# Decoder layer on one core: late maximum units of the local steps issued in pairs, value product behind them, query projection behind the value product

## The reference, cut to what matters

```python
def local_attention(x):                 # 16 heads of 8, windows of 64 tokens
    q, k, v = split(layernorm(x) @ w_qkv)
    # a chunk of 64 queries sees its own chunk and the one before it
    scores = qc @ kcat.T / 8 ** 0.5     # causal inside the window
    return softmax(scores) @ vcat @ w_out

def cross_attention(x, ctx):            # 16 heads of 8, all 256 context tokens
    q, k, v = layernorm(x) @ Wq.T + bq, ctx @ Wk.T + bk, ctx @ Wv.T + bv
    return softmax(where(mask, q @ k.T / 8 ** 0.5, -1e8)) @ v @ Wo.T + bo

x = x + local_attention(x)
x = x + cross_attention(x, ctx)
x = x + ffn(x)      # 8-bit and ternary quantised, depthwise convolution, silu
```

## Time and profile before

| what | us |
|---|---|
| median of 3 runs | 323.36 |
| lowest and highest | 322.66, 327.88 |
| the profiled execution's own time | 324.95 |
| its span, first to last instruction | 323.2 |

### The profile page before, as it was taken

One profiled execution on the slowest core, in us unless ns is written; L12 is line 12 of the kernel. 1 busy time (PEld: TensorE's weight loads), 2 busy tenths in 40 slices (PEclk: granted clock), 3 DMA queues, 4 the chain that ended last, 5 costly groups with the idle time before them and its releaser, 6 DMA issues.

```text
span 323.2 us, 8541 instructions
## 1 busy us (share of the span) xinstructions
PE 285.6 (88%) x3298; PEld 183.8 (57%) x3298; DVE 231.3 (72%) x562; ACT 164.6 (51%) x329; POOL 134.4 (42%) x216
## 2 busy tenths in 40 slices
PE   0814899999998997999999999999998999999993
PEld 0712557777775775877656656555554444544551
DVE  7758872567665665689968678786885349999675
ACT  1310016545654562655768677766777753433332
POOL 5633049656486383645869360000016413342000
PEclk9985557999999998899999999999999999999999
DMA  7278538566747653655356274300000000000001
GB/s 256 61 179 206 188 67 187 145 163 164 171 102 221 168 108 100 153 116 130 78 135 133 70 184 100 98 3 1 3 0 3 0 3 1 18 24 17 18 24 32
DMA packets 20135, 30.96 MB, mean 96 GB/s; under 512 B 2812, under 2 KB 17532, under 8 KB 18432
## 3 DMA queue, kind: packets, MB, share of 16 engines
q1 hardware_dynamic: 19368, 29.99, 37.6%
q10 hardware_dynamic: 728, 0.44, 0.5%
HBM read 16.53 MB, written 13.63 MB: 93 GB/s over the span
## 4 chain that ended last, share of the span: by engine, by line
PE 59%; DMA 15%; DVE 12%; ACT 4%; issue 4%; SPq 3%; ACTq 1%; POOL 1%; DVEq 0%
DMA KT<-stack_parts 11%; PE ps L338 9%; PE ps L303 8%; PE ps L268 7%; PE ps L403 6%; DMA QT<-mT 4%; PE ps L351 4%; PE ps L314 3%; SPq L1161 2%; PE ps L272 2%; ACT probs L588 2%; PE ps L362 2%; PE ps L286 2%; PE ps L276 2%; DVE probs L820 2%
## 5 line engine op out<-in xcount | busy, mean ns | idle before, releaser
L740 DVE TENSOR_REDUCE negm<-ps 128x2 bf16<-128x512 f32 (+1 forms) x192 | 124.1, 690 | 56.7 <-PE ps L268 24.2
L588 ACT ACTIVATE probs<-ps 128x512 f32<-128x512 f32 x192 | 105.7, 609 | 35.3 <-PE ps L314 22.9
L303 PE MATMUL ps<-QT,KT 98*128 98x512 bf16 x128 | 47.5, 382 | 4.2 <-ACT probs L588 4.0
L268 PE MATMUL ps<-KT,QT 97*128 97x256 bf16 x256 | 47.5, 272 | 2.4 <-DMA KT<-stack_parts 1.9
L403 PE MATMUL ps<-tapw,xqT 128*128 128x512 f32 x96 | 44.1, 592 | 0.0
L268 PEld LDWEIGHTS ps<-KT,QT 97*128 97x128 bf16 x256 | 23.8, 98 | 17.0 <-DVE negm L740 2.8
L338 PE MATMUL ps<-probs,V 128*32 128x256 f32 x512 | 30.9, 382 | 0.7 <-ACT probs L588 0.7
L986 POOL TENSOR_TENSOR ve<-mv,eps 128x2 f32<-128x2 f32 x8 | 1.6, 194 | 64.1 <-DVE mv L777 64.1
L1041 POOL TENSOR_SCALAR_AFFINE_SELECT probs<-probs 128x512 f32<-128x512 f32 x32 | 21.2, 661 | 14.9 <-ACT probs L588 14.9
L403 PEld LDWEIGHTS ps<-tapw,xqT 128*128 128x128 f32 x96 | 18.2, 190 | 15.0 <-issue 14.3
L626 ACT ACTIVATE probs<-ps 128x512 f32<-128x512 f32 x16 | 9.6, 597 | 33.2 <-PE ps L403 33.2
(11 more groups left out here) (134 smaller groups left out, 502.9 us busy)
## 6 DMA issues: line engine op xcount, KB each, us to landing
stack_parts<-high SPq DMA_DIRECT2D x32, 192.0 KB, 3.3
QT<-stack_parts SPq DMA_DIRECT2D x16, 384.0 KB
KT<-stack_parts SPq DMA_DIRECT2D x8, 768.0 KB
stack_parts<-mid SPq DMA_DIRECT2D x32, 128.0 KB, 3.1
stack_parts<-low SPq DMA_DIRECT2D x32, 64.0 KB, 2.1
CT<-in_ctx_t_dram SPq DMA_DIRECT2D x1, 1024.0 KB, 9.9
out_dram<-probs SPq DMA_DIRECT2D x16, 64.0 KB, 1.5
X<-in_xp_dram SPq DMA_DIRECT2D x1, 768.0 KB, 5.5
```

The costliest lines, as they stand in the source:

```text
L268: last = nc.tensor.matmul(o[:, j * S:(j + 1) * S], QT[r, s, j, pr, e * S + t * P:e * S + (t + 1) * P], KT[r, s, pr, e, :], start=True, sto ...
L303: last = nc.tensor.matmul(o.rearrange("p (j q) -> p j q", j=2), KT[r, s, pr, e, kt * P:(kt + 1) * P], QT[r, s, :, pr, e * S:(e + 1) * S], ...
L588: nc.scalar.activation(probs[:, k, :], bank(n % 3), ACT.Exp, scale=SCALE).then_inc(s_exp, 1)
L740: nc.vector.tensor_reduce(dst, src, AX.X, ALU.max, negate=True).then_inc(m_max, 1)
```

## The change

It has three parts. In local steps, where the two beats 0 and 1 (or 6 and 7) hold exactly one late maximum unit each, both beats' scores are issued first, then both masks, and then the matmuls of both units (`late_pair`, `max_late_pair`): nine such pairs, at beat 0 of steps 2 to 5 and at beat 6 of steps 1 to 5. PV_A of every local step moves from beat 6 to beat 7, so that it follows the pair, and stands ahead of `project`. In all steps `pv` of PV_B now precedes `qk_project`, and ScalarE's `o_copy` precedes `raw_copy`. VectorE, GpSimd and SyncE keep their order. No instruction is added or taken away.

```diff
-    QK, PV_B, OT, VM, OX, PV_A, Y = 1, 1, 3, 3, 5, 6, 7
+    QK, PV_B, OT, VM, OX, PV_A, Y = 1, 1, 3, 3, 5, 7, 7
...
+                def max_late_pair(n):
+
+                    for m in (n, n + 1):
+                        max_open(m)
+                        max_late_mask(m)
+                    for m in (n, n + 1):
+                        max_late_scores(m).then_inc(m_ps, 1)
...
+                def late_pair(i, k):
+
+                    ns = list(max_range(i, k)) + list(max_range(i, k + 1))
+                    return (not is_cross(i) and k in (0, 6) and len(ns) == 2 and ns[1] < 8 * B and ns[0] % 8 in (4, 6))
+
+                def beat(i, k):
+                    scores(i, k)
+                    if late_pair(i, k):
+                        return
+                    if k > 0 and late_pair(i, k - 1):
+                        max_late_pair(max_range(i, k - 1)[0])
+                        return
                     for m in max_range(i, k):
                         max_unit_mms(m)
...
                         beat(i, k)
+                        if k == at.PV_B and i >= 1:
+                            pv(i - 1, 1, bank(BX))
                         if k == at.QK and made is not None:
                             if i >= 2:
                                 pe.wait_ge(y_done, i - 1)
                             qk_project(made, bank(BY))
-                        if k == at.PV_B and i >= 1:
-                            pv(i - 1, 1, bank(BX))
...
                         exp(i, k)
+                        if k == at.PV_B and i >= 1:
+                            o_copy(i - 1, bank(BX))
                         if k == at.QK and made is not None:
                             raw_copy(made, bank(BY))
-                        if k == at.PV_B and i >= 1:
-                            o_copy(i - 1, bank(BX))
```

More of the change, by code:

```diff
@@ L258, in max_open, with max_late_mask, max_late_scores @@
                         pe.wait_ge(m_max, n - 2)
+                def max_late_mask(n):
+                    o = bank(3 + n % 3)
+                    nc.tensor.matmul(o.rearrange("p (x s) -> p x s", s=P)[:, :, W:P], identb[:],
+                                     tri_q[:].unsqueeze(1).to_broadcast([P, 4, W]),
+                                     start=True, stop=False, skip_group_check=True)
+                def max_late_scores(n):
+                    u, k = max_unit(n)
+                    o, s, e = bank(3 + n % 3), u // 2 % 3, u % 2
+                    r = slice(0, ROWS + 1)
+                    for x in range(4):
+                        pr, j = 2 * (k - 4) + x // 2, x % 2
+                        for cc in range(2):
+                            k0 = W * (1 + cc)
+                            last = nc.tensor.matmul(o[W * cc:W * cc + W, x * P:(x + 1) * P],
+                                                    QT[r, s, j, pr, e * S + k0 + W:e * S + k0 + 2 * W],
+                                                    KT[r, s, pr, e, k0:k0 + P],
+                                                    start=False, stop=(x == 3), skip_group_check=True)
+                    return last
                 def max_unit_mms(n):
@@ L278, in max_unit_mms, with scores @@
                     else:
-                        nc.tensor.matmul(o.rearrange("p (x s) -> p x s", s=P)[:, :, W:P], identb[:],
-                                         tri_q[:].unsqueeze(1).to_broadcast([P, 4, W]),
-                                         start=True, stop=False, skip_group_check=True)
-                        for x in range(4):
-                            pr, j = 2 * (k - 4) + x // 2, x % 2
-                            for cc in range(2):
-                                k0 = W * (1 + cc)
-                                last = nc.tensor.matmul(o[W * cc:W * cc + W, x * P:(x + 1) * P],
-                                                        QT[r, s, j, pr, e * S + k0 + W:e * S + k0 + 2 * W],
-                                                        KT[r, s, pr, e, k0:k0 + P],
-                                                        start=False, stop=(x == 3), skip_group_check=True)
-                    last.then_inc(m_ps, 1)
-                def beat(i, k):
+                        max_late_mask(n)
+                        last = max_late_scores(n)
+                    last.then_inc(m_ps, 1)
+                def max_late_pair(n):
[4 more added lines that the diff above has]
+                        max_late_scores(m).then_inc(m_ps, 1)
+                def scores(i, k):
                     n = before(i) + k
```

## The result

| kernel | median us | lowest, highest | runs |
|---|---|---|---|
| before | 323.6 | 322.52, 327.88 | 6 |
| changed | 327.9 | 324.78, 555.79 | 6 |

The ratio is 1.0091, 95% interval 1.0051 to 1.0131: slower by 0.9%, and within 2% of no change. 323.4 was predicted, with a range of 321.2 to 325.5. The ratio on the median of before gives 326.5, so the time lies outside.

The account below looks back on a forecast made before the run. TensorE was taken to bound the kernel (88% busy), with stack loads as gates that eat most of its saving. Gain 0.94 against costs 0.4 and 0.55 sums to 0.0, so 323.4 us, range 321.2 to 325.5.

Parts of the forecast that it names:

- Pairs: Start of step 3 on TensorE: 3.5 us instead of 3.86; over all local steps 2.7 us off TensorE's work.
- the rule quoted from the Trainium skill: TensorE: a change of tiling mode drains the engine, a change of tile within the mode does not.
- Rival C: Units still drain (nine junctions, 1.1 us) or stores keep their time, so only costs remain: 324.3 us, chance 0.10.
- PV_A in step 7: Step 7, beat 7: unit 91 waits for VectorE's take of unit 88, costing 0.4 us, between 0 and 1.0.
- The exchange in cross steps: Steps 8 to 10: later projection copies delay exp 3 and beat 6 by 0.18 us each, 0.55 in all, at most 0.8.
- On TensorE the order of two pieces costs nothing: Swapping projection and value product was taken to cost TensorE itself no time; only ScalarE's copies would cost.
- The gates: Stack loads in steps 2, 4 and 6: of TensorE's 2.7 us saving, 0.94 passes, between 0 and 2.7.
- The waits of TensorE: Expected waits for stacks: near 0.9 us in step 2, 1.7 to 1.8 in step 4, 2.1 in step 6.
- The sum: Whole kernel: -0.94 + 0.4 + 0.55 = 0.0 us, so the median stays at 323.4.
- Rival A: Copies and takes don't bind, so the 0.94 gain remains: 322.4 us, or 321.6 at best; chance 0.24.
- Its sign: From 160 us on, the trace would run over 0.7 us ahead of the earlier one.
- Rival B, the clock: Step 4's longer wait brings one more low-clock stretch, costing up to 1.7 us: 325.0 us, chance 0.21.

Follow-up runs that it names:

- lean version: Changed kernel with value product and projection exchanged in local steps only and PV_A at beat 7 only in steps 1 to 5: 322.97 us, 1.0007; again 325.88, 1.0023.
- padded changed kernel: Changed kernel with 32 small matmuls added at the very start, results unused, all stores kept: 329.27 us, 1.0117 of before.
- first repetition: Changed kernel run again unaltered on another chip for a second profile: 325.7 us, 1.0038 of before.

## Why the prediction was wrong, point by point

**Pairs, right.** Predicted 3.5 for the piece, measured 3.54; step 2-3 is 0.57 shorter (0.35 + 0.24 = 0.59 predicted). There was one idle of the loads and no drain between the two units, so the rule quoted from the Trainium skill, page "TensorEngine Tiling (Array Packing)", section "Key Properties", held in its second half too: this trace agrees. Rival C in the form of nine more drains is out.

**PV_A in step 7, right.** Predicted 0.4, measured 0.50 (12.73 against 12.23 for step 7-8 where it stands alone), with the 0.20 idle on VectorE in the row that the prediction named.

**The exchange in cross steps, the right mechanism with too small a term.** Predicted 0.18 a step and 0.55 in all; measured 0.37 and 1.1. Beat 6 waits 0.26 for exp 3, not 0.18. The rest is what the sentence "On TensorE the order of two pieces costs nothing" left out. Behind the 32-wide value product L230 holds the engine for 0.54 (167.36 to 167.90), where it took 0.43 behind 128-wide work (166.66 to 167.09 before). The upper end given for this term, 0.8, was too low as well. The same thing costs where the prediction put nothing: step 6-7, behind the gate of pair 4, has L230 and, by PV_A, the output projection (L409, 148.55 to 149.10, so 0.55, where L378 took 0.45) behind 32-wide work, and is 0.21 longer. Costs behind that gate are therefore 1.8, not 0.95.

**The gates: forecast in part, and the gain isn't in the medians.** The prediction let 0.94 through, as a chain from TensorE over the take, the split and the stores to the loads. In the first profile the load of QT for pair 3 went out 0.34 earlier (0.35 predicted) and KT of pair 4 1.10 earlier (0.94), in the two later ones 1.07 and 2.08 earlier. Here is SyncE's queue, which answers to the earlier trace rows:

```profile
90.61 0.80 SPq L1208 DMA_DIRECT2D QT<-stack_parts  x2
```

KT of pair 3 came at its old time in the first profile, since its row still took as long as QT's data: 4.92 (5.38 before). In the later ones it went out 0.59 and 0.90 earlier. The waits of TensorE were not those worked out: at the stack of step 2 1.24 us, and none in the later profiles (0.9 predicted); in step 4 1.53, 1.28 and 1.49 (1.7 to 1.8); in step 6 1.10, 2.72 and 1.08 (2.1).

The gate of pair 5, in the first profile alone, was not foreseen. Before, QT was loaded at 141.92, the row went out at 146.84 and KT at 149.25. Here QT goes out at 142.98, late behind the stores, and the row at 143.83 close behind it, takes 5.09, and KT goes out at 148.94: 3 us won by TensorE up to there are 0.31 at the transfer. In the later profiles QT was out at 141.66 and 139.80, the row 3.1 behind it, and nothing waited. The prediction read the gates up to 130 us and took what passed the last of them as won.

**The sum: the step that failed.** Predicted -0.94 + 0.4 + 0.55. The two costs, which nothing behind them hides, were 0.50 + 1.10 = 1.6 us, in every profile with both parts: 7 to 11 took 56.73 in both repetitions, against 55.14. With the 0.21 of step 6-7 this is 1.8, 0.6% of 323. The three ratios of the changed kernel, 1.0091, 1.0038 and 1.0078, have a mean of 1.0069. The version without these costs was level twice (1.0007, 1.0023), and on the chip where both ran its interval (up to 1.0031) lies below the changed kernel's (from 1.0048). So the costs are shown to make most of the loss. The other half of the failure is the gain of 0.94. Had it been there, the lean version would have stood near 0.997, and both its intervals lie above that (from 0.9983 and 0.9990). What the prediction named as rival C (323.4 + 0.94 = 324.3), with a chance of 0.10, is close to this, with its costs at 1.8 rather than 0.94.

Where the gain went isn't shown. The profiles of the changed kernel have it: from the turn in step 1 to that in step 7 they take 77.4, 79.2 and 77.3 us, and the kernel before 80.8, its low clock of up to 1.7 with it. But they are of quick executions, and that of before, the only one, is of an execution 1.35 us above the median of 323.6. Rival A, that the costs don't bind, is out, since they are in every profile. Its sign, a trace over 0.7 us ahead from 160 us on, was there at the turn in step 9 (171.33, 172.22 before) and gone at that in step 10 (186.29, 186.82).

**Rival B, the clock, not decided.** Step 4's wait grew to 1.53 and no low stretch followed it in the changed kernel; the one behind step 6 is in none of its three profiles. So it isn't borne out where it was put. But behind the stack of step 6 it may be what eats the gain. The lean version has a low stretch there in each of its three profiles (one padded), behind waits of 1.93, 2.46 and 2.70 us, for 3.3, 6.8 and 6.8 us; the kernel before had 1.90 and 3.4. Its step 5-6 took 15.93, 17.62 and 17.91, against 16.03. The second of these, wait and window:

```profile
126.76 1.03 PE L292 MATMUL ps<-KT,QT 97*128 97x256 bf16 x4 [2.46 <-DMA KT<-stack_parts]
...
125.90:132.70 6.80, 5.94 (x80) 4.34 (x81) 1.30 (x2) 1.56 (x4) 1.78 (x4) 0.51 0.01 3
```

The padded changed kernel, whose profiled execution (328.46) was no quick one, has a low stretch there too, behind 2.62 us, and 16.68 in step 5-6, where the changed kernel's three have 13.55, 15.17 and 13.54. No run kept this wait away with all else equal, so the clock stays a rival.

**Open.** Why the first six runs lay at 327.9 where later chips gave 325.7 and 325.6, and how much of the differences between executions is the clock. All three profiles of the unpadded changed kernel caught its quicker executions (324.78, 324.67, 322.86 where the medians were 327.9, 325.7, 325.64), so its slower ones were not seen. The single parts are also smaller than what a median tells here: the exchange undone (1.0041, then 1.0017) shows by its steps that 1.1 us came back, not by its times.

## What to carry to other kernels

What an engine wins ahead of a gate that a transfer sets is waited off unless the transfer comes earlier too, and a longer wait can bring the low clock; read the gates to the end of the kernel, with the row and the stack at each, and in more than one profile, before counting a gain. Here one of three profiles had a gate that the others lacked. Costs behind the last gate are paid in full (56.73 against 55.14), so a reordering that saves among local steps should be confined to them. And two pieces that change places on one engine change their neighbours' tile widths there, and what stands next in line on the engine that copies them.

## What was not expected of the hardware

- A small load is slow behind a large one though it goes by another queue: the row took 2.09 and 2.47 us when issued over 4 us behind QT, and 4.92, 5.09 and 5.38 when issued 1.4, 0.9 and 0.6 us behind it.
- TensorE can stand still 0.5 to 3.3 us within a row of equal matmuls while a piece of program arrives; 32 small matmuls more at the start moved the longest away (1.0046 to 0.9957). Where a piece came while the last stores of pair 5 were on their way, the load behind them was late too (2.50 to 3.32 us after the last store's issue, not 1.58).
- A float matmul group with 128-wide weights took 0.54 us behind 32-wide ones, rather than 0.43 behind 128-wide ones.
- Of the low clock, by the waits of TensorE for data between 50 and 160 us in 19 profiles: none of the 14 from 1.21 to 1.72 us was followed by a granted clock under 1.00, while 26 of the 29 from 1.85 to 4.74 us were, at about 0.50 (1.2 GHz). Fifteen of the 29 are the wait for the first stack near 52 us, where the clock fell before the wait was over; of the other 14, 11 were followed. The three exceptions had 2.09, 2.57 and 2.72 us. The last of them is the only long wait past 60 us in the changed kernel's three profiles (first repetition, step 6):

```profile
126.10 0.61 PE L288 MATMUL ps<-KT,QT 97*128 97x256 bf16 x4 [2.72 <-DMA KT<-stack_parts]
```

and the clock stayed up behind it (window):

```profile
126.20:129.60 3.40, 3.40 (x83) 2.71 (x83) 1.40 (x3) 1.34 (x4) 0.55 (x1) 1.00 0.02 5
```

It waited as long as others that were followed by a low clock; what tells them apart wasn't found.
